# Two pairs of projections as 64-row tiles in a fused cross-attention and feed-forward kernel, with other work moved around them

## The reference

```python
def attention(x, ctx, pos):                      # x: 16 x 256 x 512, ctx: 16 x 256 x 256
    q = rope(layernorm(x) @ Wq, pos)             # 32 heads of 16
    k, v = split(ctx @ Wkv); k = rope(k, pos)
    w = softmax(q @ k.T / 4)                     # per head, 256 x 256
    return (w @ v) @ Wout + bout
x = x + tanh(g_xattn) * attention(x, ctx, pos)
h = layernorm(x)
y = square(relu(h @ up)) @ down + (h @ expert_weight) * sum(top2(h @ gate_w))
x = x + tanh(g_ffn) * (layernorm(y) * gamma + beta)
```

## Time and profile before

| | us |
|---|---|
| median of 3 runs | 1567.92 (1567.05 to 1567.99) |
| the profiled execution | 1566.75 |
| its span | 1564.9 |
| PE busy | 1515.9 (97%) |
| DVE busy | 980.2 (63%) |
| ACT busy | 635.0 (41%) |
| POOL busy | 337.9 (22%) |

### The profile page before, as it was taken

How to read it: one execution, slowest core, us unless ns; L and a number is a source line. 1 busy time by engine, 2 the same in 40 slices (tenths; PEclk the granted TensorE clock), 3 DMA queues, 4 the chain that set the end, 5 groups by cost and what they waited for, 6 DMA issues and landing times.

```text
span 1564.9 us, 25920 instructions
## 1 busy us (share of the span) xinstructions
PE 1515.9 (97%) x9498; PEld 1125.0 (72%) x9498; DVE 980.2 (63%) x1416; ACT 635.0 (41%) x962; POOL 337.9 (22%) x406
## 2 busy tenths in 40 slices
PE   7789999999999999979999999999999999999997
PEld 6556666666666666646787888878888888788886
DVE  7788888888888888755655436435354264453524
ACT  4365665655555666665432222222222222222221
POOL 5323233333333333112101002001020020110202
PEclk9699999999999999999999999999999999999999
DMA  6645555555555555544411001101011010010101
GB/s 174 142 98 141 134 137 138 131 142 139 135 135 143 127 127 136 121 134 120 147 61 35 27 21 47 35 15 47 21 35 47 1 54 27 22 40 21 55 0 41
DMA packets 80623, 131.11 MB, mean 84 GB/s; under 512 B 21624, under 2 KB 35064, under 8 KB 80504
## 3 DMA queue, kind: packets, MB, share of 16 engines
q1 hardware_dynamic: 80504, 129.48, 32.4%
HBM read 51.17 MB, written 16.78 MB: 43 GB/s over the span
## 4 chain that ended last, share of the span: by engine, by line
PE 88%; DVE 7%; issue 2%; POOL 1%; ACT 1%; DMA 0%; SPq 0%; POOLq 0%; DVEq 0%; ACTq 0%
PE pP L1113 17%; PE pT L1113 11%; PE pA L1314 11%; PE pO L1113 11%; PE pB L1314 11%; PE pA L1211 7%; PE pO L1239 7%; PE pB L1227 3%; PE pM L1113 3%; DVE mneg L1534 3%; PE pP L1120 2%; PE pM L1120 2%; PE pT L1195 1%; PE pM L1281 1%; PE pM L1187 1%
## 5 line engine op out<-in xcount | busy, mean ns | idle before, releaser
L1534 DVE TENSOR_REDUCE mneg<-pA 128x4 f32<-128x1024 f32 x250 | 305.7, 1223 | 97.7 <-PE pA L1211 93.2
L1012 ACT ACTIVATE probs<-pB 128x1024 f32<-128x1024 f32 x249 | 255.8, 1027 | 213.2 <-PE pB L1227 203.3
L811 POOL TENSOR_SCALAR var_eps<-meanvar 128x1 f32<-128x1 f32 x96 | 34.6, 360 | 986.1 <-DVE meanvar L1416 985.9
L1637 DVE TENSOR_TENSOR relu<-relu 128x512 f32<-128x512 f32 x128 | 88.4, 690 | 252.3 <-ACT hid L1066 252.3
L1314 PE MATMUL pA<-dn,hid 128*128 128x512 f32 x768 | 197.1, 392 | 1.7 <-DVE hid L1639 1.5
L1314 PE MATMUL pB<-dn,hid 128*128 128x512 f32 x768 | 195.0, 389 | 0.0
L1113 PE MATMUL pP<-fT,up 128*128 128x512 f32 x768 | 188.5, 394 | 0.0
L1113 PE MATMUL pO<-fT,up 128*128 128x512 f32 x768 | 184.7, 389 | 0.0
L1314 PEld LDWEIGHTS pA<-dn,hid 128*128 128x128 f32 x768 | 142.9, 188 | 34.4 <-DVE hid L1639 5.1
L1113 PEld LDWEIGHTS pO<-fT,up 128*128 128x128 f32 x768 | 144.0, 188 | 30.3 <-issue 0.4
L1314 PEld LDWEIGHTS pB<-dn,hid 128*128 128x128 f32 x768 | 144.1, 188 | 30.0
(11 more groups left out here) (200 smaller groups left out, 1989.8 us busy)
## 6 DMA issues: line engine op xcount, KB each, us to landing
stk<-kT SPq DMA_DIRECT2D x180, 128.0 KB, 2.9
stq<-qT SPq DMA_DIRECT2D x180, 128.0 KB, 2.9
fres<-x_scratch SPq DMA_DIRECT2D x34, 256.0 KB, 2.9
xin<-x SPq DMA_DIRECT2D x32, 256.0 KB, 2.9
numer<-av_s SPq DMA_DIRECT2D x128, 64.0 KB, 2.4
xres<-x SPq DMA_DIRECT2D x32, 256.0 KB, 2.9
x_scratch<-xres SPq DMA_DIRECT2D x32, 256.0 KB, 2.4
out<-y_s SPq DMA_DIRECT2D x32, 256.0 KB, 2.0
```

The source lines that it names most:

```text
L811: nc.gpsimd.tensor_scalar_add(var_eps[:], meanvar[:, 1:2], EPS).then_inc(ve_made, 1)
L1012: nc.scalar.activation(probs[:, s % 4, :, :, :].rearrange("p a b s -> p a (b s)"), psum[:, :, :], ACT.Exp).then_inc(exp_done, 1)
L1534: nc.vector.tensor_reduce(mneg[par][:, :, 2 * u:2 * u + 2].rearrange("p t q -> p q t"), psum[:, :, :].rearrange("p q (t k) -> p q t k", t= ...
L1637: nc.vector.tensor_tensor(r[:], r[:], r[:], ALU.mult).then_inc(sq_made, 1)
```

## The change

Four projections of an iteration are computed in two pairs with half-height tiles. In a pair, the two products write different banks. In a first part the one takes rows 0 to 63 of its chunks and the other rows 64 to 127, alternating matmul by matmul; in a second part they change places. PE waits between the parts until the first is complete (`rows_done`). V0 is paired with the second half of Q0: the first part stands between the two logits of step 4, the second behind them. The second half of O1 is paired with V1: the first part behind the logits of step 14, before `times_v`, the second behind the logits of step 15. A pair has 24 matmuls in place of 12.

Other jobs move: `Q0<` from step 2 to 3, X1 from 5 to 6, `Q1<` from 7 to 8. Within steps 3, 8, 10 and 12 the order changes. On DVE the second statistics and `ln_apply` of an iteration move from steps 2 and 3 to 3 and 4, the reciprocals from 14 and 5 to 12 and 4. V0 and V1 change banks. In phase 2 `fres` has four buffers: SP loads all four tiles ahead of the stores of a block, and for the last block POOL adds `g_beta` to all four before it makes any 1/std.

```diff
-    2: ("Q0<", "b0"),
-    3: ("m1", "Q0"),
-    4: ("V1",),
-    5: ("kT0", "X1"),
-    6: (),
-    7: ("K1", "Q1<"),
-    8: ("Q1", "b1"),
+    2: ("b0",),
+    3: ("Q0<", "m1"),
+    4: ("V0", "Q0"),
+    5: ("kT0",),
+    6: ("X1",),
+    7: ("K1",),
+    8: ("Q1<", "b1", "Q1"),
...
-    14: ("V0",),
-    15: ("O1",),
+    14: (),
+    15: ("O1", "V1"),
...
+PAIRS = (
+    (("V0", "Q0"), (4, "first logits"), (4, "second logits")),
+    (("O1", "V1"), (14, "second logits"), (15, "second logits")),
+)
-RECIPROCALS = {14: 0, 5: 1}
+RECIPROCALS = {12: 0, 4: 1}
...
+            def paired(n, i, par, swapped):
+                if swapped:
+                    pe.wait_ge(rows_done, pair_number(n, i))
+                sides = []
...
+                    rows = slice(HALF_ROWS, P) if (k == 1) != swapped else slice(0, HALF_ROWS)
...
+                for c in range(CC):
+                    for a, w in PASSES:
...
+                        for psum, rows, half, bank, lhs, rhs, _ in sides:
+                            at = c + (CC if half == 1 else 0)
+                            last = nc.tensor.matmul(psum[:, :], lhs(a, at)[rows, :], rhs(w, at)[rows, :],
+                                                    start=opens and half != 1, stop=closes and half != 0)
...
-                    if s == 2 and within(i + 2) and not first:
+                    if s == 3 and within(i + 2) and not first:
                         ln_statistics(i + 2, 1)
-                    elif s == 3 and within(i + 2) and not first:
+                    elif s == 4 and within(i + 2) and not first:
                         ln_apply(i + 2, 1)
...
             for u in range(UT):
-                for_output(NB - 1, u, 2 * UT * NB - UT + u + 1)
+                add_beta(NB - 1, u)
+            for u in range(UT):
+                ffn_inv_std(2 * UT * NB - UT + u + 1)
```

More of the change, by code:

```diff
@@ L141, in first_maxima, with pair_at, pair_number @@
     return isinstance(b, int) and b == 0 and u < STEPS - DELAY
+def pair_at(n, i):
+    names = PAIRS[n][0]
+    return names if within(i) and all(live(x.rstrip("<"), i) for x in names) else ()
+def pair_number(n, i):
+    order = sorted(range(len(PAIRS)), key=lambda k: PAIRS[k][1])
+    return (sum(bool(pair_at(k, j)) for j in range(i) for k in order)
+            + sum(bool(pair_at(k, i)) for k in order[:order.index(n) + 1]))
 def before(names, i):
@@ L341, in flamingo_gated @@
         gt_raw = sb2("gt_raw", [P, KC, NEXP])
+        fres += [sb2(f"fres{k}", [P, D]) for k in range(2, UT)]
         second.close()
@@ L359, in flamingo_gated @@
         f_lo = sem("f_lo")
+        rows_done = sem("rows_done")
         o_done = sem("o_done")
@@ L433, in flamingo_gated @@
         z_made = sem("z_made")
-        fres_in = [sem(f"fres_in{k}") for k in range(2)]
+        fres_in = [sem(f"fres_in{k}") for k in range(UT)]
         fres_made = sem("fres_made")
@@ L674, in first_tiles @@
                         sp.wait_ge(*stack_in(x, half, B - 1))
-                sp.wait_ge(taken[BANK["V0"]], number("V0", B - 1))
+                for name in ("V0", "V1"):
+                    sp.wait_ge(taken[BANK[name]], number(name, B - 1))
                 for t in range(TT):
@@ L737, in fblock @@
                     for u in range(UT):
[L738 to L744, removed]
+                        sp.dma_start(fres[u][:], x1_d[(j - 1) * UT + u]).then_inc(fres_in[u], INC)
+                    for u in range(UT):
                         n = (j - 1) * UT + u
@@ L823, in split_ctx @@
                 if some(b - 1):
-                    pool.wait_ge(done[BANK["V0"]], number("V0", b - 2))
+                    for name in ("V0", "V1"):
+                        pool.wait_ge(done[BANK[name]], number(name, b - 2))
                 alone(pool)
@@ L896, in ffn_inv_std, with add_beta @@
                 inv_std(NT + count)
[L898 to L903, removed]
+            def add_beta(j, u):
+                pool.wait_ge(fres_in[u], INC * (j + 1))
+                nc.gpsimd.tensor_tensor(fres[u][:], fres[u][:], g_beta[:], ALU.add).then_inc(fres_made, 1)
             pool.wait_ge(gb_made, 2)
@@ new lines, in paired @@
+            def paired(n, i, par, swapped):
+                if swapped:
+                    pe.wait_ge(rows_done, pair_number(n, i))
+                sides = []
+                for k, name in enumerate(PAIRS[n][0]):
+                    half, name = (0, name[:-1]) if name[-1] == "<" else (1 if name in CUT else None, name)
+                    b, at, bank = i + LAG[name], (par + LAG[name]) % 2, BANK[name]
+                    if not swapped:
+                        if half != 1 and some(number(name, b) - 1):
+                            pe.wait_ge(taken[bank], number(name, b) - 1)
+                        inputs_of(name, b, half)
+                    rows = slice(HALF_ROWS, P) if (k == 1) != swapped else slice(0, HALF_ROWS)
+                    sides.append(({"P": pP, "M": pM, "T": pT}[bank], rows, half, bank) + factors(name, b, at))
+                for c in range(CC):
+                    for a, w in PASSES:
+                        opens = not swapped and c == 0 and (a, w) == PASSES[0]
+                        closes = swapped and c == CC - 1 and (a, w) == PASSES[-1]
+                        for psum, rows, half, bank, lhs, rhs, _ in sides:
+                            at = c + (CC if half == 1 else 0)
+                            last = nc.tensor.matmul(psum[:, :], lhs(a, at)[rows, :], rhs(w, at)[rows, :],
+                                                    start=opens and half != 1, stop=closes and half != 0)
+                            if closes and half != 0:
+                                last.then_inc(done[bank], 1)
+                if not swapped:
+                    last.then_inc(rows_done, 1)
@@ L1162, in compute, with pieces @@
+            def pieces(place, i, par):
+                for n, (_, upper, lower) in enumerate(PAIRS):
+                    for swapped, at in enumerate((upper, lower)):
+                        if at == place and pair_at(n, i):
+                            paired(n, i, par, bool(swapped))
             def compute(name, b, par, psum, half=None):
@@ L1166, in compute @@
                     last = turn(psum, lambda c: xn[:, c * P:(c + 1) * P])
[L1167 to L1179, removed]
+                elif name[0] in "QKVO":
+                    inputs_of(name, b, half)
+                    last = product(psum, *factors(name, b, par), half)
                 elif name[0] in "qk":
@@ L1233, in times_v @@
                 if g == 0:
-                    pe.wait_ge(taken[BANK["V0"]], number("V0", b))
+                    for name in ("V0", "V1"):
+                        pe.wait_ge(taken[BANK[name]], number(name, b))
                 if some(GROUPS * b + g):
@@ L1260, in iteration @@
                         logits_a(i, par % 2, STEPS - DELAY + s)
+                    pieces((s, "first logits"), i, par)
                     if within(i):
                         logits_b(i, par % 2, s)
+                    pieces((s, "second logits"), i, par)
                     if s in VALUES and within(i):
@@ L1266, in iteration @@
                         times_v(i - 1, (par + 1) % 2, GROUPS - 1)
+                    together = {x for n in range(len(PAIRS)) for x in pair_at(n, i)}
                     for name in names_at(i, s):
-                        job(name, i, par)
+                        if name not in together:
+                            job(name, i, par)
                     if planned(tile_at, i, s) is not None:
@@ L1619, in norm_y @@
                                                ALU.mult).then_inc(z_made, 1)
+            def norm_y(j, u, count):
+                n = UT * j + u
+                y = y_s[:, u, :]
+                centre_y(j, u, count)
                 dve.wait_ge(z_made, n + 1)
```

25 lines of the change are left out of this document (20 added, 5 removed), and 4 rows, old and new, of the table BANK.

## The result

The changed kernel is slower by 0.3%: 1572.28 us median of 7 runs (1569.52 to 1573.98) against 1567.61 for the kernel before, in 7 runs on the same chip (1565.22 to 1567.99). The ratio is 1.003, 95% interval 1.0018 to 1.0042. Forecast was 1568 with a range of 1556 to 1574. So the time lies in the range, 4.3 us above the forecast and just outside the forecast's own 1565 to 1571.

A forecast was written before the change was run, and what follows sets the result against it. PE was taken to bound phase 1, except steps 2 to 6, where DVE does. Plus 4.0, minus 0.5, minus 0.7 and minus 2.9 sum to minus 0.1 us, giving 1568 us for the median, range 1556 to 1574.

The forecast's parts named there:

- steps 7 to 1, an iteration: Stretch of an iteration where PE alone decides; pairing and moved jobs change it by minus 0.41 us.
- steps 2 to 6, an iteration: Stretch where DVE decides; instructions held by POOL lengthen it from 12.82 to 13.54 us, plus 0.72.
- an undisturbed iteration, x 13: Both stretches together, plus 0.31 us an iteration, in full for iterations 1 to 13: plus 4.0.
- iteration 0: First iteration: first pair alone, no reciprocals, b0 of an element before; minus 0.5 us.
- iteration 14: Iteration with the second pair alone; minus 0.7 us.
- the end, from the last exponential: Last three output tiles lose 0.97 us each because POOL's g_beta additions come earlier; minus 2.9 us.
- PE's costs of the pairs: Steps 4, 14 and 15: two half-height 512-column matmuls beside each other take 0.225 us a slot.
- the list: DVE's instructions timed from step 2's start, with POOL's holds; step 7 starts at 13.54 us.
- a loss of 0.73 for the cast: Step 4: what the reciprocals' cast loses to POOL's exclusive port lock, against 0.2 if speed were merely shared.
- The rival by which the hold isn't there: Steps 2 to 6 without any hold of DVE: 1551 us; part of the faster rival, chance 0.38.
- the covers "about 0.3 is left": Slack before PE's b0 in step 2, as m0, stack loads and scatter shift later; costed at nothing.
- The slower rival with K0 and the other covers: K0 waits for ctx, or step 5 and 6 waits lengthen: 0.3 us an iteration, 1572 us; chance 0.12.

The follow-up runs named there:

- e6_both: Changed kernel with two swaps in POOL's list: K0's rope sum before 1/std, Q0's rope sum before rest_av; 1556.78 us, ratio 0.9941.
- e7: e6_both with the first reciprocals of an iteration back in step 14; 1556.55 us, ratio 0.9937.
- e9: e6_both without the pairs, the four projections at full height; 1567.68 us, ratio 1.0013.
- e10: e1_tail with both of POOL's swaps (K0's rope sum before 1/std, Q0's before rest_av); 1573.14 us, ratio 1.0037.
- e1_tail: Kernel before with the fres part alone: four buffers, g_beta added to all four last tiles before any 1/std; 1563.84 us, ratio 0.9985.
- e8: e6_both with the reciprocals in steps 14 and 5, as in the kernel before; 1604.12 us, ratio 1.023.
- e5: Changed kernel with one swap in POOL's list: K0's rope sum before 1/std; 1558.85 us, ratio 0.995.
- e3_recip14: Changed kernel with the first reciprocals of an iteration back in step 14; 1569.3 us, ratio 1.0024.

## Why the prediction was right in kind and 4 us low

The terms of the sum, as differences of the two profiled executions:

| term | predicted | measured |
|---|---|---|
| steps 7 to 1, an iteration | -0.41 | -0.37 |
| steps 2 to 6, an iteration | +0.72 | +0.61 |
| an undisturbed iteration, x 13 | +4.0 | +3.0 (+0.23 each) |
| longer iterations among these 13 | 0 | +2.9 |
| iteration 0 | -0.5 | -0.1 |
| iteration 14 | -0.7 | +1.9 (37.71 to 39.58) |
| iteration 15, up to the last exponential | 0 | +1.5 (33.10 to 34.59) |
| opening, up to the first `logits_b` | 0 | +1.2 (62.74 to 63.89) |
| the end, from the last exponential | -2.9 | -3.0 |
| sum | -0.1 | +7.2 |

The medians differ by 4.7 and not by 7.2: the profiled execution of the kernel after was its longest of seven. The opening is 62.6 to 62.7 in e6_both, e7 and e9, which have the change, and 63.76 in e10, which has no pairs, so the 1.2 there is scatter. So is a part of the rows of iterations 14 and 15: e1_tail, whose phase 1 is that of the kernel before, has 38.25 and 33.63 for iterations 14 and 15, each 0.5 more. The 1.0 that the prediction has too much for the 13 iterations hides a third of the 2.9 that it has too little for the long ones among them.

**Right.** PE's costs of the pairs: 0.23 us from pair to pair (0.225 taken), 42.30 an iteration (42.37). `ln_apply` at 1.28 (1.20 taken) and its end 0.28 behind POOL's; the cast held, at 0.88 (0.6 to 0.8 forecast, though the list itself makes it 0.84, from 8.80 to 9.64); PE's wait moved to step 6. Two numbers there have no working. The list has `rest_av` ready at 8.20 and lets it run from 8.31; it ran from 8.33, behind ACT. And a loss of 0.73 for the cast stands in no sum; the list gives 0.65, and 0.69 was measured. The Trainium skill, "SBUF — State Buffer", section "SBUF: two separate sides", calls the shared pair an exclusive lock for a whole instruction, between GpSimd and those VectorE instructions that run in a two-port mode or have two inputs in SBUF. `ln_apply`, the casts and the subtraction of e8 agree, since each ends 0.04 to 0.28 us behind POOL's instruction however late it started. The rival by which the hold isn't there is what e5 and e6 made of it: 1551 was given for that, 1556.8 is what it brings. Of the difference, 0.15 an iteration is PE's own list for steps 2 to 6: 12.24 by the prediction, 12.39 in e6_both (2.09 + 3.85 + 1.96 + 2.25 + 2.24). In its trace the rest stands in iterations 1 and 9 (0.5 and 0.9 over the others), in 0 and 14 (0.5 and 1.3 over the prediction) and in 15 (1.4 over the kernel before).

**The step that failed** is the sentence "Iteration 0 has the first pair alone ...: minus 0.5. Iteration 14 has the second pair alone: minus 0.7", and with it the covers "about 0.3 is left" at b0. I priced the first and last iterations by PE's list alone, while in the last ones waits for DVE and for small DMAs decide: minus 0.7 was taken for iteration 14, plus 1.9 came. At b0 the cover was not enough in iterations 1, 9 and 10 (0.7, 0.7 and 0.4 us, e3_recip14 above). In iteration 14 nothing is prepared for a later element, PE has little work, and the reciprocals of step 4 came before their sums (timeline of the kernel after):

```profile
668.96 0.55 DVE L1545 RECIPROCAL den<-den 64x64 f32<-64x64 f32 x1 [1.67 <-DMA den<-av_s]
...
671.17 0.50 PE L1271 MATMUL pA<-stk,stq 48*128 48x256 f32 x4 [1.97 <-DVE mneg L1599]
```

Before, they stood a step later, in 5 (step 5 took 1.83 there, 3.70 now). At the start of step 6 the logits' weight loads had stood idle for 0.58 us before, and for 2.47 now; in e8, with the reciprocals in step 5 again, for 0.60. In iteration 15 PE waits for the maxima's DMA, as it did before for 1.9:

```profile
711.50 0.79 PE L1287 MATMUL pB<-stq,stk 50*128 50x256 f32 x4 [2.57 <-DMA stq<-low]
```

Behind such idle time the granted clock is lower (stretches of the kernel after; the column behind POOL's is the clock):

```profile
671.00:677.00 6.00, 3.21 (x40) 1.98 (x40) 3.79 (x4) 3.45 (x4) 0.84 (x1) 0.98 0.40 110
677.00:681.00 4.00, 3.82 (x28) 2.06 (x28) 1.82 (x2) 1.02 (x1) 1.65 (x2) 0.50 0.88 197
...
708.00:714.00 6.00, 1.72 (x20) 0.80 (x8) 2.35 (x5) 3.46 (x5) 1.69 (x3) 0.74 0.46 143
714.00:720.00 6.00, 5.84 (x38) 3.08 (x42) 2.07 (x4) 2.92 (x5) 1.93 (x3) 0.50 0.47 93
```

PE was busy for 3.21 of 6 us and 1.72 of 6, and right behind each the clock is 0.50, 1.2 GHz. But the kernel before has this dip in the same places (0.60 for 669 to 675 us, 0.55 for 706 to 712). Over the whole of iteration 14 the mean granted clock is 0.91 in both kernels and PE is busy for 32.3 and 32.5 us, so there the clock is no part of the difference: what grew is PE's idle time, from 5.4 to 7.1. In iteration 15 both grew, the idle time from 6.1 to 7.2 and the busy time from 27.0 to 27.4, at a mean clock of 0.90 and 0.85. How much of these waits each edit brings stays open. The kernels with pairs have iteration 14 between 37.5 (e3_recip14) and 39.8, but without them it goes from 37.7 to 39.9 (e9) too, in one trace each.

The slower rival with K0 and the other covers ("K0 waits for ctx, or the waits of step 5 and 6 are longer": 1572) gives the time that was measured, but not for its reason: K0 did not wait, and the waits of steps 5 and 6 are shorter than forecast.

## What to carry to other kernels

Before an instruction of DVE that reads and writes SBUF is moved, lay POOL's instructions beside it: here a hold cost up to 1.0 us, a second one came where POOL had its next instruction ready (e8), and what was late by one hold was late enough to meet another (the changed kernel). Two swaps in POOL's list are worth more here (15 us) than the pairs that the change was about (some 11 when nothing hides them). Price the first and last iterations of a loop by their own waits and not as the middle ones less what is missing.

## What was not expected of the hardware

- Two half-height matmuls of 64 rows and 512 columns that accumulate into different banks run beside each other at 0.23 us a pair, as fast as one of full height (0.223). Each half-height weight load takes 0.18 to 0.19 us in the records, and 24 of them to a pair showed in no interval, unless it is in the 0.09 behind the wait for `rows_done`. A load of 128 rows takes 0.19 as well (`LDWEIGHTS` of 128x128, mean 188 ns). The Trainium skill, "TensorE: Matmul & The Clock Gate", section "LDWEIGHTS (loading the stationary operand)", says that rows don't count in a load, and these agree; the length in the records is above the 0.107 that the prediction took from its formula. The 1.3 us a pair that it would have cost unhidden did not come.
- Not every DVE instruction is held by POOL. In e10 the reciprocal (SBUF to SBUF) took 0.53 with POOL busy from its start to its end, and in e5 the maxima of step 3, read from PSUM, took 1.22 beside the rope sum of K0, as they do elsewhere. Held were `ln_apply` (1.28 for 0.52), the cast (up to 1.01 for 0.19) and the subtraction of the low part (1.22 for 0.22).
- The cast ends 0.04 to 0.05 us behind POOL's instruction, the subtraction in e8 0.09 and `ln_apply` 0.28 behind it.
- PE's idle time did not always bring the clock down: in e8 the same wait ahead of step 7 was followed by a clock of 1.00 in iteration 8 and of 0.55 in iteration 9, where the step took 1.3 us more.
